# Self-attention with the score matrix built twice: once for its maxima, once with keys on partitions

## The chip, the cores and the metric

One NeuronCore of a Trainium2 chip runs the whole program in one launch. The metric is the device time of one execution in microseconds. The engines are PE (TensorE: matmuls, with its weight loads shown apart), DVE (VectorE), ACT (ScalarE), POOL (GpSimd) and SP (SyncE, which here only issues DMAs).

## The reference

Two blocks follow each other on x of shape (2, 256, 32, 32), in fp32. The first is a deformable attention with a bias network and an MLP; the change leaves it alone. The second is plain self-attention over the 1024 pixels of each image, 8 heads of width 32, so 16 (image, head) pairs:

```python
xf = transpose(x.reshape(B, C, N), (0, 2, 1))            # N = 1024
q, k, v = split((xf @ W_qkv + b_qkv).reshape(B, N, 8, 96), 3, axis=-1)
attn = softmax(einsum('bihd,bjhd->bijh', q, k) * SCALE, axis=2)
res  = einsum('bijh,bjhd->bihd', attn, v).reshape(B, N, 256)
res  = res @ W_out + b_out + xf
```

## The kernel before

Each engine has an instruction stream written out by hand; semaphores tie them together. The first attention, its bias network and the MLP fill the span up to 1027 us. The second attention is what the change rewrites. Its stages before:

1. V product (L1026, added to the bias by DVE in L741): 16 blocks of 128 pixels, all 256 value columns, two fp32 matmuls a block.
2. q and k projections (L1038): 8 products n (which = q or k, t = a block of 128 channels), each of four fp32 512-column matmuls. ACT takes the fp32r rounding of each (L531, semaphore f_hi) and DVE the rest (L767, f_lo). SP writes both parts to DRAM (`send_parts`, L299) and later fetches, for a head, the 32 rows of a part several times under each other (`load_head`, L303 and L304: 8 DMAs of 128 KB), so that one product over 128 rows gives hi*hi + hi*lo + lo*hi + lo*lo. DVE splits V into three bf16 parts meanwhile (`v_part`).
3. The loop: `Fori` over 8 pairs of heads, 16 units in each, 128 units in all. A unit is 128 queries (on partitions) against 1024 keys. PE makes the scores (`scores`, L1047, two 512-column fp32r matmuls), DVE their negated row maximum (`maxes`, L773), ACT the exponential with that bias (L535), PE eight 128x128 transposes of the probabilities (`turn`, L1055), ACT, DVE and POOL the fp16 high and low parts of the result (L540, L543, L776, L779, L390), PE 16 small matmuls with V (`weigh`, L1063), whose last column holds the sum, DVE its reciprocal (L786), ACT the scaling (L550), POOL two adds (L395, L397).
4. PE transposes the results back (L1102), ACT copies them (L574), PE does the output projection (L1113, 32 records), DVE adds bias and input (L814), SP stores (L327).

A matmul of two fp32 operands appears in the trace as two records; a fp32r one as one. Where the output lies in 32 of 128 partitions ("128*32" in a row), four such matmuls run side by side in the array: the layer-3 product of the bias network (L907) is of that form.

PSUM has 8 banks of 512 fp32. Before, scores of unit u lie in banks 2(u%2) and the next, so they are double buffered.

Of the kernel before, what the change touches and what calls it, by code (L numbers as in the profile page):

```python
# [7 lines left out]
P = 128  # L8
# [7 lines left out]
KD = 8  # L16
# [41 lines left out]
def build(nc, d, out):  # L58
# [5 lines left out]
    with ctx:  # L64
# [14 lines left out]
        k_d = dram("k_d", [2, G * D, N], fp32)  # L79

# [8 lines left out]
        qw = sb("qw", [P, CT, P])  # L89
        kw = sb("kw", [P, CT, P])  # L90
        vw = sb("vw", [P, CT, P])
        outw = sb("outw", [P, CT, C])
        m1 = sb("m1", [P, CT, 4 * C])
# [6 lines left out]
        conv = sb("conv", [P, T * 9, KD])  # L100
        gel = sb("gel", [P, T * 9, KD])
# [23 lines left out]

        gb = m1[:, :, :]
# [34 lines left out]
        def v(name, i=0, n=1):  # L161
# [32 lines left out]
        st_in = [sem("st_in0"), sem("st_in1")]  # L194
        sc_ready, mx_ready, pr_ready, pT_ready, pTh_ready, pTl_ready, oo_ready, oo_saved = (
            sem(x) for x in ("sc_ready", "mx_ready", "pr_ready", "pT_ready", "pTh_ready", "pTl_ready", "oo_ready", "oo_saved"))
        pF_ready, pFh_ready, pFl_ready = sem("pF_ready"), sem("pFh_ready"), sem("pFl_ready")
        v_done = sem("v_done")
        sums_column, o_sum, o_done = sem("sums_column"), sem("o_sum"), sem("o_done")
        rT_ready, rT_saved, fin_ready, fin_saved, stored = (  # L200
            sem(x) for x in ("rT_ready", "rT_saved", "fin_ready", "fin_saved", "stored"))
# [26 lines left out]
        def _(sp):  # L228
# [946 lines left out]
```

## Time and profile before

| | us |
|---|---|
| median of 3 runs | 1402.4 (1402.36 to 1404.89) |
| profiled execution, its own time | 1401.21 |
| its span in the profile | 1399.0 |
| PE busy | 1302.2 (93%) |
| ACT busy | 967.6 (69%) |
| DVE busy | 921.5 (66%) |
| POOL busy | 748.9 (54%) |
| V product begins (L1026) | 1027.11 |
| first scores (L1047) | 1073.88 |
| output projection begins (L1113) | 1381.88 |

Times inside the profile are counted from the start of the span; 2.2 us of the execution lie outside it. A busy PE is not a PE at its peak: the durations of matmuls overlap, so what one costs is the distance between starts. "issue" in a chain is time in which an engine waited for nothing that the profile shows.

### The profile page before, as it was taken

To read this page: it belongs to the slowest core of one execution; us is meant where nothing else is said; L and a number is where in the kernel's file an instruction comes from. 1 tells how busy PE (TensorE), PEld (TensorE's weight loads), DVE (VectorE), ACT (ScalarE), POOL (GpSimd) and SP (SyncE) were. 2 spreads that over 40 slices of the span, in tenths; PEclk is the share of its full clock that TensorE was granted. 3 is DMA by queue.
4 is the path that set the end of the run, shared out by engine and by line. 5 is a ranking of instruction groups with operands and counts; after the bars stand their busy time and mean duration, and the time that the engine had idled before them with its cause. 6 is when DMAs were issued, how large, how long until landed. Compare 5 with 4: busy or idle time off the path is not lost.

```text
span 1399.0 us, 29958 instructions
## 1 busy us (share of the span) xinstructions
PE 1302.2 (93%) x11666; PEld 616.0 (44%) x11666; DVE 921.5 (66%) x1270; ACT 967.6 (69%) x1263; POOL 748.9 (54%) x681
## 2 busy tenths in 40 slices
PE   3169999999999999999999998799997999999998
PEld 2132222222222222222222226444454888888885
DVE  6876666666666666666666657410037999999995
ACT  3377777777777777777777773332204999999994
POOL 4166666666666666666666652200000767777772
PEclk9579999999999999999999999999999999999999
DMA  2141110111011101110111000000007222212211
GB/s 69 54 134 31 31 32 2 31 31 32 2 31 32 29 4 32 31 26 7 31 32 23 9 1 1 1 0 0 0 29 272 62 60 60 54 45 52 60 30 60
DMA packets 19922, 53.27 MB, mean 38 GB/s; under 512 B 4642, under 2 KB 7330, under 8 KB 19668
## 3 DMA queue, kind: packets, MB, share of 16 engines
q1 hardware_dynamic: 19824, 51.92, 14.1%
q8 instruction: 70, 1.15, 0.4%
q14 instruction: 24, 0.20, 0.0%
q10 hardware_dynamic: 4, 0.01, 0.0%
HBM read 40.95 MB, written 10.95 MB: 37 GB/s over the span
## 4 chain that ended last, share of the span: by engine, by line
PE 80%; DVE 11%; issue 3%; ACT 2%; POOL 2%; DMA 1%; SPq 1%; DVEq 0%; ACTq 0%; POOLq 0%
PE ps L898 31%; PE ps L907 17%; PE ps L889 5%; DVE aneg L773 5%; PE ps L1055 4%; PE ps L1063 4%; PE ps L1004 4%; PE ps L1014 4%; PE ps L1047 3%; DVE conv L620 2%; PE ps L1038 1%; DVE big L776 1%; POOL big L355 1%; PE ps L1026 1%; PE ps L991 1%
## 5 line engine op out<-in xcount | busy, mean ns | idle before, releaser
L898 PE MATMUL ps<-big,w 64*64 64x512 f32 x4096 | 483.5, 589 | 0.0
L479 ACT ACTIVATE big<-ps 128x1024 f32<-128x1024 f32 x256 | 262.0, 1023 | 179.0 <-PE ps L898 179.0
L674 DVE TENSOR_SCALAR big<-big 128x1024 f32<-128x1024 f32 x256 | 177.8, 694 | 263.8 <-POOL big L370 263.8
L668 DVE TENSOR_TENSOR big<-qpad,ps 128x1024 f32<-128x1024 f32 x256 | 311.0, 1215 | 7.8 <-ACT ps L458 5.4
L370 POOL TENSOR_TENSOR big<-qpad 128x1024 f32<-128x1024 f32 x128 | 244.5, 1910 | 133.2 <-PE ps L898 68.6
L370 POOL TENSOR_TENSOR big<-qpad,V 128x1024 f32<-128x1024 f32 x128 | 244.5, 1910 | 129.7 <-PE ps L898 73.5
L479 ACT ACTIVATE big<-ps,vec 128x1024 f32<-128x1024 f32 x256 | 284.0, 1109 | 0.0
L390 POOL TENSOR_TENSOR big<-BT,big 128x512 f16<-128x512 f32 x129 | 150.4, 1166 | 248.0 <-DVE big L776 248.0
L907 PE MATMUL ps<-big,w3s 128*32 128x512 f32 x2048 | 246.2, 598 | 1.3 <-ACT big L479 1.3
L898 PEld LDWEIGHTS ps<-big,w 64*64 64x64 f32 x4096 | 146.6, 133 | 205.9 <-issue 112.6
L773 DVE TENSOR_REDUCE aneg<-ps 128x1 f32<-128x1024 f32 x131 | 158.3, 1209 | 6.0 <-PE ps L1047 5.7
L535 ACT ACTIVATE big<-ps,aneg 128x1024 f32<-128x1024 f32 x130 | 148.5, 1142 | 6.0 <-DVE aneg L773 5.3
L1055 PE MATMUL ps<-ident,big 128*128 128x128 f32 x1032 | 136.3, 274 | 3.8 <-DVE big L779 3.8
L907 PEld LDWEIGHTS ps<-big,w3s 128*32 128x32 f32 x2048 | 53.5, 109 | 181.7 <-ACT big L479 92.2
L1055 PEld LDWEIGHTS ps<-ident,big 128*128 128x128 f32 x1032 | 121.1, 141 | 23.2 <-DVE big L779 5.7
L1063 PE MATMUL ps<-BT,big 128*128 x2048 | 115.6, 208 | 1.1
L1063 PEld LDWEIGHTS ps<-BT,big 128*128 128x128 f16 x2048 | 99.0, 97 | 21.3 <-issue 10.3
L889 PE MATMUL ps<-S,wl 57*64 57x512 bf16 x1024 | 102.3, 389 | 1.5 <-ACT vs L474 1.5
L1047 PE MATMUL ps<-h1l,h1h 128*128 128x512 f32 x262 | 94.5, 443 | 6.8 <-DMA h1l<-k_d 5.2
L889 PEld LDWEIGHTS ps<-S,wl 57*64 57x64 bf16 x1024 | 29.5, 105 | 144.7 <-ACT big L479 80.7
L779 DVE SCALAR_TENSOR_TENSOR big<-ps,big 128x512 f16<-128x512 f32 x129 | 89.1, 691 | 0.8 <-ACT big L543 0.4
L540 ACT ACTIVATE BT<-ps 128x512 f32<-128x512 f32 x129 | 79.1, 613 | 4.0 <-PE ps L1055 4.0
(140 smaller groups left out, 1116.5 us busy)
## 6 DMA issues: line engine op xcount, KB each, us to landing
raw<-s_f SPq DMA_DIRECT2D x32, 512.0 KB, 6.1
h1h<-q_d SPq DMA_DIRECT2D x64, 128.0 KB, 3.0
h1l<-k_d SPq DMA_DIRECT2D x64, 128.0 KB, 3.1
q_d<-XN SPq DMA_DIRECT2D x8, 512.0 KB, 2.6
k_d<-XN SPq DMA_DIRECT2D x8, 512.0 KB, 2.6
X<-in_x SPq DMA_DIRECT2D x2, 1024.0 KB, 6.3
out<-X SPq DMA_DIRECT2D x8, 256.0 KB, 2.0
m<-grid_d SPq DMA_DIRECT2D x1, 1024.0 KB, 4.6
```

The costliest lines, as they stand in the source:

```text
L370: pool.tensor_tensor(h1[m % HRING].rearrange("p (y a b) -> p y a b", y=2, b=W), u.unsqueeze(2).to_broadcast(shape), a[:, :, HALF // W * hf ...
L390: pool.tensor_tensor(PTL[u % 2][:, 0:HALF], PF[u % 2], PTH[u % 2][:, 0:HALF], ALU.subtract).then_inc(pFl_ready, 1)
L479: act.activation(h2[m % H2RING], z2[m % ZRING], ACT.Relu, bias=v("cb2") if m % 2 else 0.0).then_inc(h2_ready, 1)
L535: act.activation(PR[u % 2], bank(2 * (u % 2), 2), ACT.Exp, bias=aneg[u % 2][:, :]).then_inc(pr_ready, 1)
L668: dve.tensor_tensor(h1[m % HRING].rearrange("p (y a b) -> p y a b", y=2, b=W), u.unsqueeze(2).to_broadcast(shape), b[:, :, HALF // W * hf: ...
L674: dve.tensor_scalar(h1[m % HRING], h1[m % HRING], 0.0, None, ALU.max).then_inc(h1_ready, 1)
L773: dve.tensor_reduce(aneg[u % 2][:, :], bank(2 * (u % 2), 2), AX.X, ALU.max, negate=True).then_inc(mx_ready, 1)
L889: pe.matmul(z2[m % ZRING][CH * y:CH * (y + 1), HALF * x:HALF * (x + 1)], wl1[CH * x:CH * x + KROWS, 2 * w + y, :], S[CH * x:CH * x + KROWS ...
L898: last = pe.matmul(z2[m % ZRING][CH * y:CH * (y + 1), HALF * x:HALF * (x + 1)], w2[CH * x:CH * (x + 1), :], h1[m % HRING][CH * x:CH * (x + ...
L907: last = pe.matmul(zb[32 * k:32 * (k + 1), :], w3s[:, a:a + 32], h2[(m + k // 2) % H2RING][:, HALF * (k % 2):HALF * (k % 2 + 1)], start=(m ...
L1055: last = pe.transpose(bank(4 + hf)[:, P * i:P * (i + 1)], PR[u % 2][:, P * jt:P * (jt + 1)], ident[:, :])
L1063: last = pe.matmul(bank(6 + u % 2)[:, 0:VW], pT[u % 2][:, P * jt:P * (jt + 1)], V3[:, 2 * k + u // NK, jt, :], start=(jt == order[0] and p ...
```

## The change

The transposes of the probabilities, the fp16 parts, the bf16 parts of V and the final transposes go. The second attention becomes this, over 128 slots (16 heads x 8 blocks), all written out with no `Fori`:

- `along(x)`: scores with queries on partitions (query i of block `it` is number 8i + it, so the stationary operand is read with a stride of 8), three stacked products (96 rows) in place of four, always in banks 0 and 1. It serves only for the negated maxima (`maxes`), kept as 8 columns a head.
- POOL splits a head's maxima into a fp32r part and the rest; SP writes them to DRAM and reads them back as two rows of 1024 (`move_max`), rows 96 and 97 of the head's query operand; the key operand holds ones there.
- `across(s)`: the same scores again, keys on partitions, 98 rows, so that the product already has the maximum subtracted; banks 2 and 3 or 4 and 5. ACT takes the exponential straight from there into a ring of 6 (`PT`).
- `weigh(p)`: 8 fp32 matmuls of 256 columns, four side by side, first with V (128x32), then with ones (128x32), which gives the sums. `divide(n)`: a reciprocal of 128x256 and a multiplication for each head, whose result SP places with four DMAs (`place_head`).
- PE's order in slot s: `across(s)`, `along(s + 13)`, and in odd slots `weigh(s - 3)` and `weigh(s - 2)`. Thirteen `along` stand ahead of slot 0, the first eight with two V blocks (`value`) before each.
- Heads 0, 1 and 2 are loaded at first (6 DMAs each); head n + 2 is loaded in iteration n of SP's loop, after the last `across` of head n - 1.
- The projections come ahead of the V product now, and SP sends only four of the eight parts before it loads heads. In the first block the tiles qw, kw, conv and gel share space with others, and the late weights are fetched after k_ready.

```diff
-Q_STACK, K_STACK = [0, 0, 1, 1], [0, 1, 0, 1]
-VW = 3 * D + 1
-PSCALE = 2.0 ** 12
+Q_STACK, K_STACK = [0, 0, 1], [0, 1, 0]
+ROWS = D * len(Q_STACK)
+HEADS3, PRING, AHEAD_MAX = 3, 6, 13
+QUARTER = N // 4
 WS_POOL = 4
-UNITS = 2 * NK
+SLOTS = G * NK
 
...
-        QS = [h1h[:, 2 * i:2 * i + 2, :].rearrange("p a b -> p (a b)") for i in range(2)]
+        QS = [h1h[:, 2 * i:2 * i + 2, :].rearrange("p a b -> p (a b)") for i in range(2)] + [qk3[:, 0, :]]
+        KS = [h1l[:, 2 * i:2 * i + 2, :].rearrange("p a b -> p (a b)") for i in range(2)] + [qk3[:, 1, :]]
+        PT = [big[:, 4 + i, :] for i in range(PRING)]
+        OT = [big[:, 10, QUARTER * i:QUARTER * (i + 1)] for i in range(2)]
+        orec = [big[:, 10, QUARTER * i:QUARTER * (i + 1)] for i in (2, 3)]
+        amax = [sb(f"amax{i}", [P, NK]) for i in range(HEADS3)]
+        mparts = [sb(f"mparts{i}", [P, 2, NK], fp32r) for i in range(HEADS3)]
...
-            for n in range(6):
+            def load_head(n):
+                i = n % HEADS3
+                for r in range(len(Q_STACK)):
+                    sp.dma_start(QS[i][D * r:D * (r + 1), :].bitcast(fp32), q_d[Q_STACK[r], D * n:D * (n + 1), :]).then_inc(st_in[i], 16)
+                    sp.dma_start(KS[i][D * r:D * (r + 1), :].bitcast(fp32), k_d[K_STACK[r], D * n:D * (n + 1), :]).then_inc(st_in[i], 16)
+            def move_max(n):
+                sp.wait_ge(m_lo, n + 1)
+                sp.dma_start(m_d[n].rearrange("a (q t) -> q a t", t=NK), mparts[n % HEADS3][:, :, :].bitcast(fp32)).then_inc(m_out, 16)
+                sp.wait_ge(m_out, 16 * (n + 1))
+                sp.dma_start(QS[n % HEADS3][ROWS:ROWS + 2, :].bitcast(fp32), m_d[n]).then_inc(m_in, 16)
+            def place_head(n):
+                sp.wait_ge(o_done, n + 1)
+                row, t = D * (n % HP), n // HP
+                for c in range(4):
+                    sp.dma_start(rT[row:row + D, t, QUARTER * c:QUARTER * (c + 1)], OT[n % 2][D * c:D * (c + 1), :]).then_inc(rT_in, 16)
+            for n in range(4):
                 send_parts(n)
             for i in range(2):
-                sp.wait_ge(parts_out[i], 32 * 3)
-            load_head(0, 0)
-            load_head(1, 1)
-            for n in range(6, 2 * T):
+                sp.wait_ge(parts_out[i], 32 * 2)
+            for n in range(HEADS3):
+                load_head(n)
+            for n in range(4, 2 * T):
                 send_parts(n)
             for i in range(2):
                 sp.wait_ge(parts_out[i], 32 * T)
-            with sp.Fori(0, G // 2 - 1) as k:
-                sp.wait_ge(sc_ready, UNITS * k + NK)
-                load_head(0, 2 * k + 2)
-                sp.wait_ge(sc_ready, UNITS * k + 2 * NK)
-                load_head(1, 2 * k + 3)
-            sp.wait_ge(sc_ready, UNITS * (G // 2 - 1) + NK)
-            sp.sem_inc(st_in[0], 16 * 2 * HP)
+            move_max(0)
+            for n in range(1, G):
+                if n + 2 < G:
+                    if n >= 2 or n + 2 >= HEADS3:
+                        sp.wait_ge(st_ready, NK * (n + 2 - HEADS3 + 1))
+                    load_head(n + 2)
+                move_max(n)
+                place_head(n - 1)
+            place_head(G - 1)
...
+            pool.memset(ones[:, :], 1.0).then_inc(ones_ready, 1)
+            pool.wait_ge(ones_ready, 1)
+            for i in range(HEADS3):
+                pool.tensor_copy(KS[i][ROWS:ROWS + 2, :], ones[ROWS:ROWS + 2, 0:1].to_broadcast((2, N))).then_inc(ones_ready, 1)
+            pool.wait_ge(ones_ready, 1 + HEADS3)
+            for n in range(G):
+                pool.wait_ge(mx_ready, NK * (n + 1))
+                if n >= HEADS3:
+                    pool.wait_ge(m_out, 16 * (n - HEADS3 + 1))
+                hi, lo = (mparts[n % HEADS3][:, a, :] for a in range(2))
+                pool.tensor_copy(hi, amax[n % HEADS3][:, :]).then_inc(m_hi, 1)
+                pool.wait_ge(m_hi, n + 1)
+                pool.tensor_tensor(lo, amax[n % HEADS3][:, :], hi.bitcast(fp32), ALU.subtract).then_inc(m_lo, 1)
...
+            for s in range(SLOTS):
+                act.wait_ge(st_ready, s + 1)
+                if s >= PRING:
+                    act.wait_ge(pv_done, s - PRING + 1)
+                act.activation(PT[s % PRING], bank(2 + 2 * (s % 2), 2), ACT.Exp).then_inc(pr_ready, 1)
...
+            def maxes(x):
+                n, it = x // NK, x % NK
+                dve.wait_ge(sc_ready, x + 1)
+                if it == 0 and n >= HEADS3:
+                    dve.wait_ge(m_lo, n - HEADS3 + 1)
+                dve.tensor_reduce(amax[n % HEADS3][:, it:it + 1], bank(0, 2), AX.X, ALU.max, negate=True).then_inc(mx_ready, 1)
+            def divide(n):
+                dve.wait_ge(pv_done, NK * (n + 1))
+                dve.reciprocal(orec[n % 2], bank(6 + n % 2)[:, QUARTER:2 * QUARTER]).then_inc(rec_done, 1)
+                dve.wait_ge(rec_done, n + 1)
+                if n >= 2:
+                    dve.wait_ge(rT_in, 64 * (n - 1))
+                dve.tensor_tensor(OT[n % 2], bank(6 + n % 2)[:, 0:QUARTER], orec[n % 2], ALU.mult).then_inc(o_done, 1)
...
+            for x in range(NK):
+                value(2 * x)
+                value(2 * x + 1)
+                maxes(x)
+            for x in range(NK, SLOTS + 2 * NK):
+                if x < SLOTS:
+                    maxes(x)
+                n = (x - NK - AHEAD_MAX - 1) // NK
+                if n >= 0 and (x - NK - AHEAD_MAX - 1) % NK == 0:
...
+            def along(x):
+                n, it = x // NK, x % NK
+                if it == 0:
+                    pe.wait_ge(st_in[n % HEADS3], 96 * (n // HEADS3 + 1))
+                if x >= 1:
+                    pe.wait_ge(mx_ready, x)
+                for hf in range(2):
+                    last = pe.matmul(bank(hf), QS[n % HEADS3][0:ROWS, it:it + NK * (P - 1) + 1:NK],
+                                     KS[n % HEADS3][0:ROWS, HALF * hf:HALF * (hf + 1)], start=True, stop=True)
+            def across(s):
+                n, kt = s // NK, s % NK
+                if kt == 0:
+                    pe.wait_ge(m_in, 16 * (n + 1))
+                if s >= 2:
+                    pe.wait_ge(pr_ready, s - 1)
+                for hf in range(2):
+                    last = pe.matmul(bank(2 + 2 * (s % 2) + hf), KS[n % HEADS3][0:ROWS + 2, P * kt:P * (kt + 1)],
+                                     QS[n % HEADS3][0:ROWS + 2, HALF * hf:HALF * (hf + 1)], start=True, stop=True)
+                last.then_inc(st_ready, 1)
+            def weigh(s):
+                n, kt = s // NK, s % NK
+                if kt == 0 and n >= 2:
+                    pe.wait_ge(o_done, n - 1)
+                pe.wait_ge(pr_ready, s + 1)
+                for a, w in enumerate((V[:, n, kt, :], ones[:, :])):
+                    for c in range(4):
+                        last = pe.matmul(bank(6 + n % 2)[D * c:D * (c + 1), QUARTER * a:QUARTER * (a + 1)], w,
+                                         PT[s % PRING][:, QUARTER * c:QUARTER * (c + 1)],
+                                         start=(kt == 0 and a == 0), stop=(kt == NK - 1), skip_group_check=True)
+                last.then_inc(pv_done, 1)
+            for x in range(NK):
+                value(2 * x)
+                value(2 * x + 1)
+                along(x)
+            for x in range(NK, AHEAD_MAX):
+                along(x)
+            pe.wait_ge(vv_saved, 2 * NK)
+            pe.wait_ge(ones_ready, 1 + HEADS3)
+            for s in range(SLOTS + 2):
+                if s < SLOTS:
+                    across(s)
+                if s + AHEAD_MAX < SLOTS:
+                    along(s + AHEAD_MAX)
+                if s % 2 == 1:
+                    for p in (s - 3, s - 2):
+                        if p >= 0:
+                            weigh(p)
+            pe.wait_ge(mx_ready, SLOTS)
+            pe.wait_ge(pr_ready, SLOTS)
```

## Rows read from the trace of the kernel before

**Rows 1.** Page, chain that ended last: shares of the span by engine.

```profile
PE 80%; DVE 11%; issue 3%; ACT 2%; POOL 2%; DMA 1%; SPq 1%; DVEq 0%; ACTq 0%; POOLq 0%
```

**Rows 2.** Windows, loop of 128 units: length, busy per engine (instructions), clock, DMA.

```profile
1085.00:1370.00 285.00, 280.64 (x3221) 242.22 (x3219) 275.15 (x497) 277.19 (x496) 200.87 (x370) 1.00 0.22 52
```

**Rows 3.** Timeline inside the loop: start, duration, engine, line, operation.

```profile
1203.11 0.71 PE L1047 MATMUL ps<-h1l,h1h 128*128 128x512 f32 x2
...
1203.31 1.13 ACT L535 ACTIVATE big<-ps,aneg 128x1024 f32<-128x1024 f32 x1
...
1203.66 1.03 PE L1055 MATMUL ps<-ident,big 128*128 128x128 f32 x8
...
1203.91 1.20 DVE L773 TENSOR_REDUCE aneg<-ps 128x1 f32<-128x1024 f32 x1
...
1204.64 0.87 PE L1063 MATMUL ps<-BT,big 128*128 x16
...
1205.34 0.71 PE L1047 MATMUL ps<-h1l,h1h 128*128 128x512 f32 x2
```

**Rows 4.** Timeline, end of a pair of heads, where DVE waited for scores.

```profile
1360.18 0.72 PE L1047 MATMUL ps<-h1l,h1h 128*128 128x512 f32 x2
...
1360.94 1.23 DVE L773 TENSOR_REDUCE aneg<-ps 128x1 f32<-128x1024 f32 x1 [0.32 <-PE ps L1047]
```

**Rows 5.** Timeline, bias network: a 128*32 burst and what follows it.

```profile
500.52 1.92 PE L907 MATMUL ps<-big,w3s 128*32 128x512 f32 x16
502.37 0.41 PE L889 MATMUL ps<-S,wl 57*64 57x512 bf16 x4
```

**Rows 6.** DMA issues: out<-in, count, size of one, median us from issue to landing.

```profile
h1h<-q_d SPq DMA_DIRECT2D x64, 128.0 KB, 3.0
...
q_d<-XN SPq DMA_DIRECT2D x8, 512.0 KB, 2.6
...
vec<-in_vecs SPq DMA_DIRECT2D x1, 41.0 KB, 1.9
...
grid_d<-gxy SPq DMA_DIRECT2D x1, 8.0 KB, 2.5
```

**Rows 7.** Timeline, start of the second attention.

```profile
1027.11 14.08 PE L1026 MATMUL ps<-qpad,X 128*128 128x256 f32 x64 [0.84 <-DVE X L736]
...
1056.11 1.28 DVE L767 SCALAR_TENSOR_TENSOR XN<-ps,vec,XN 128x1024 fp32r<-128x1024 f32 x1 [1.01 <-ACT XN L531]
...
1066.97 0.35 SPq L303 DMA_DIRECT2D h1h<-q_d  x1
...
1073.88 2.04 PE L1047 MATMUL ps<-h1l,h1h 128*128 128x512 f32 x4 [5.23 <-DMA h1l<-k_d]
1074.32 0.90 SPq L299 DMA_DIRECT2D q_d<-XN  x2
```

**Rows 8.** Windows around the wait before the first scores.

```profile
1068.50:1071.00 2.50, 0.15 (x1) 0.00 (x0) 1.49 (x2) 2.29 (x2) 0.00 (x0) 1.00 0.94 252
...
1078.00:1080.00 2.00, 2.00 (x9) 1.70 (x9) 1.20 (x1) 0.96 (x2) 0.00 (x0) 0.50 1.03 416
```

**Rows 9.** Timeline, end of the first attention: a shorter idle time of PE.

```profile
892.66 1.09 PE L978 MATMUL ps<-ident,big 128*128 128x128 f32 x4 [2.30 <-POOL big L377]
```

**Rows 10.** Window right behind it.

```profile
893.00:894.00 1.00, 0.75 (x4) 0.34 (x2) 0.82 (x2) 1.00 (x2) 0.07 (x1) 0.50 0.00 0
```

**Rows 11.** Groups by form: busy us, mean ns, idle before.

```profile
L1026 PE MATMUL ps<-qpad,X 128*128 128x256 f32 x64 | 14.1, 381 | 0.8 <-DVE X L736 0.8
...
L786 DVE RECIPROCAL arec<-ps 128x1 f32<-128x1 f32 x128 | 20.2, 158 | 0.0
...
L713 DVE RECIPROCAL srec<-ssum 128x8 f32<-128x8 f32 x16 | 3.1, 196 | 0.0
...
L741 DVE TENSOR_TENSOR big<-ps,bv 128x256 f32<-128x256 f32 x16 | 6.8, 425 | 7.8 <-PE ps L1026 7.8
```

**Rows 12.** Timeline, the output projection at the end.

```profile
1381.88 13.90 PE L1113 MATMUL ps<-XN,qpad 128*128 128x512 f32 x32
```

More of the change, by code:

```diff
@@ L124, in build @@
         vs = sb("vs", [P, T, 2, 2 * D])
+        conv, gel = (big[:, i, 0:T * 9 * KD].rearrange("p (a b) -> p a b", b=KD) for i in (10, 11))
         gb = m1[:, :, :]
@@ L736, in _, with value @@
                     dve.scalar_tensor_tensor(xs, bank(4 + r % 4), v("mlp_b2", ct), xs, ALU.add, ALU.add).then_inc(x2_ready, 1)
-            for n in range(2 * NK):
+            def value(n):
                 b, jt = n // NK, n % NK
@@ L1020, in _ @@
             wv = wqkv[:, :, :].rearrange("p t (k n) -> p t k n", k=3)
-            for n in range(2 * NK):
-                b, jt = n // NK, n % NK
-                if n >= 4:
-                    pe.wait_ge(vv_saved, n - 3)
-                for kt in range(CT):
-                    last = pe.matmul(bank(4 + n % 4)[:, 0:C], X[:, CT * b + kt, P * jt:P * (jt + 1)], wv[:, kt, 2, :],
-                                     start=(kt == 0), stop=(kt == CT - 1))
-                last.then_inc(vv_ready, 1)
             pe.wait_ge(qw_scaled, 2)
@@ L1040, in _ @@
                 last.then_inc(p_ready, 1)
-            def scores(u):
-                i, it = u // NK % 2, u % NK
-                for jh in range(2):
-                    last = pe.matmul(bank(2 * (u % 2) + jh), QS[i][:, P * it:P * (it + 1)], KS[i][:, HALF * jh:HALF * (jh + 1)],
-                                     start=True, stop=True)
-                last.then_inc(sc_ready, 1)
-            def turn(u, hf):
-                for i in range(4):
-                    jt = 4 * hf + i
-                    last = pe.transpose(bank(4 + hf)[:, P * i:P * (i + 1)], PR[u % 2][:, P * jt:P * (jt + 1)], ident[:, :])
-                last.then_inc(pT_ready, 1)
@@ L1058, in weigh @@
-            def weigh(u, k):
-                order = list(range(4, NK)) + list(range(4))
-                for jt in order:
-                    for pT in (PTH, PTL):
-                        last = pe.matmul(bank(6 + u % 2)[:, 0:VW], pT[u % 2][:, P * jt:P * (jt + 1)],
-                                         V3[:, 2 * k + u // NK, jt, :],
-                                         start=(jt == order[0] and pT is PTH), stop=(jt == order[-1] and pT is PTL))
-                last.then_inc(oo_ready, 1)
@@ L1094, in _, with value @@
[L1094 to L1105 removed]
+            def value(n):
+                b, jt = n // NK, n % NK
+                if n >= 4:
+                    pe.wait_ge(vv_saved, n - 3)
+                for kt in range(CT):
+                    last = pe.matmul(bank(4 + n % 4)[:, 0:C], X[:, CT * b + kt, P * jt:P * (jt + 1)], wv[:, kt, 2, :],
+                                     start=(kt == 0), stop=(kt == CT - 1))
+                last.then_inc(vv_ready, 1)
```

186 lines of the change are left out of this document (15 added, 171 removed).

## The prediction

> **What bounds the kernel now.** I read the page's chain first: 80% of what ended last is PE [rows 1], and up to 1027 us the change touches none of it. So I read the second attention alone. The windows of its loop show PE busy 280.6, ACT 277.2 and DVE 275.2 of 285 us at clock 1.00 [rows 2]: three engines are full together. In the timeline the scores of two units start at 1203.11 and 1205.34 [rows 3]; over the loop a unit takes about 2.2 us. PE spends them as 0.55 us from scores to transposes, 0.98 on transposes and 0.70 on the product with V, by starts [rows 3]. That is the price to beat, 2.2 us a unit, 128 times; a rewrite that only lifts ACT and DVE gains nothing, if PE or a chain of waits then takes 2.4.
>
> **The change part by part.** I rebuild the timeline from 1027.11, where the V product begins [rows 7], and add the terms.
>
> *Start.* The projections move ahead of the V product, so they begin 13.9 us earlier. The rest of part 3 (L767, started at 1056.11, 1.28 us) ends then at 1043.5 instead of 1057.4 [rows 7]; its DMA lands 2.6 us later [rows 6], at 1046.1. SP now loads three heads: 18 DMAs. Before, 16 of them stood between 1066.97 and 1074.32 [rows 7], 0.46 us each, so 18 hold SP for 8.3 us, till 1054.4, and the parts 4 to 7 are queued behind them. The data: 18 x 128 KB at the 252 GB/s of such loads [rows 8] flow till 1055.8 at the earliest, I take 1057, then four half-megabyte parts at about 416 GB/s [rows 8] until 1062, landed at 1063. ACT reuses the buffer of part 5 for part 7 only then, about 1.1 us, and DVE's rest takes 1.28 [rows 7]. PE waits for all rests: it starts on V at 1065.4, after an idle time of 10 us. Without that jam it would be 1057; with faster loads 1062.
>
> *The thirteen `along` ahead.* V costs 14.08 us for 16 blocks [rows 7, 11], 0.88 a block, and a pair of fp32r matmuls 0.43 (two records that together last 0.71, the last of them with its latency) to 0.55 (the distance to the next form [rows 3]); I take 0.45. Eight rounds of two blocks and one `along`: 8 x 2.2 = 17.7. The banks 0 and 1 are single now, so an `along` waits for the maximum of the one ahead: scores start at 1360.18, DVE at 1360.94, for 1.23 us [rows 4], and with some 0.05 to the release that is a chain of 2.04 us from `along` to `along`. Five more: 10.2. PE restarts cold: before, after 5.23 us of idleness [rows 7] it still ran at clock 0.50 between 1078 and 1080, up to 6 us later [rows 8]. Of 6 us at half speed 3.1 are lost, gaps and edges estimated. Slot 0 begins at 1065.4 + 17.7 + 10.2 + 3.1 = 1096.4.
>
> *A pair of slots.* `weigh` has the form of L907, whose burst of 16 records of 512 columns holds PE for 1.85 us including the change of array form [rows 5]; two `weigh` are 32 records of half the length, so 1.85 again (bounds 1.72, with no overhead, and 2.0, with the overhead of L907 for each group of four). PE's order per pair is: `along` (odd x), `across`, `along` (even x), two `weigh`, `across`. The first `along` and the second stand 2.04 us apart by the chain of the maximum, although PE has only one `across` of 0.45 to do between them: about 1.1 us of PE idle. After the second come 0.45 + 1.85 + 0.45 = 2.75 us, which covers its own maximum. The period is 2.04 + 2.75 = 4.8, with changes of form 4.85: 2.43 us a slot, more than the 2.2 before. Bounds: 4.66 (1.72 for the weights) and 5.14 (0.55 per pair of matmuls, 2.0). ACT has one exponential a slot, 1.13 us [rows 3], and hides. 115 slots also hold an `along`: 57.5 x 4.85 = 278.9 (bounds 268 to 296). The last 13 have none: 6.5 x 2.75 = 17.9. Pair 0 has no `weigh` and one pair stands after the last slot: +1.0.
>
> *Head boundaries.* Slot 8n needs `m_in`(n), the maxima of its head. They are known six slots earlier, but SP issues `move_max`(n) behind `load_head`(n + 2), which waits for `across`(8n - 1): the slot just before. From its end: six issues of 0.46 = 2.8 us; the maxima out, an 8 KB DMA of 256 short pieces, like grid_d 2.5 us; back in again 1.9 to 2.5 [rows 6]. That is 7.2 to 7.8 if the small DMA passes the six loads. The last load is issued at 2.5 and lands 3.0 later, at 5.5 [rows 6]; if the small one follows it, it lands at 6 to 7 and slot 8n starts at 8 to 9. I take 8.2. PE's own cover from the end of `across`(8n - 1): the rest of the 2.04 chain, an `along` and two `weigh`, 3.3 us. Stall 4.9 us (bounds 4.0 and 5.7). n = 1 to 13 have it; heads 14 and 15 have no load ahead of `move_max`, so SP is not held. 13 x 4.9 = 63.7 (52 to 74).
>
> The Trainium skill, in "DMA: Bandwidth & Descriptors", "Queues, rings and completion order", says that descriptors of SP's DMAs are consumed in ring order on each DMA engine. By that rule the maxima wait behind the loads and the upper half of my bounds holds (about +0.5 us each, +6 in all); no row shows a small DMA behind loads.
>
> *The clock after each stall.* After 5.23 us idle PE came back at 0.50 [rows 7, 8], and after 2.30 us as well (restart 892.66, 0.50 in the window behind it) [rows 9, 10]. A stall of 4.9 may therefore end at half speed. In the 6 us behind it the pair loses 2 to 2.5 us (the matmuls double, the idle of the maximum chain takes part of it back). I count 1.6 us a boundary: 13 x 1.6 = 20.8 (0 to 33).
>
> *`divide`.* It follows the maximum of an even x, waits for the `weigh` of its head and so sits just ahead of the next maximum, with no slack. Reciprocals of 1 and 8 elements take 158 and 196 ns [rows 11], 5.4 ns an element, so 256 cost about 1.5 us; the multiplication is like L741, 0.42 [rows 11]. It starts at 4.65 of the period, ends at 6.7, and the maximum that could have begun at 5.65 is 1.05 late: 14 heads x 1.05 = 14.7 (0, if the reciprocal runs like L741, to 24).
>
> The Trainium skill, "VectorE: DVE Perf Modes", "First, the fixed hardware budget", has the reciprocal as an iterated divide with a repeat count of 8, which speaks against the change. Read as 8 cycles of its 0.96 GHz for each element that would be an estimate of 2.1 us in place of 1.5 and 14 x 0.6 = 8 us more; the two short rows fit neither value well.
>
> *End.* The output projection starts at 1381.88, 17.1 us ahead of the span's end [rows 12]. The first image's four groups (6.9 us) hide the last `divide` (2.0), its four issues and a landing. The 8 transposes that stood ahead of it, some 3.6 us, are gone; that is in the sum since I start from the last `weigh`. POOL's two operations of 128x8 lie in the six slots of lead. The earlier edits (shared tiles, late weights after k_ready) I put at nothing: the raw load of the next group is needed tens of us later; if not, 1 to 2 us.
>
> *Sum.* 1096.4 + 278.9 + 17.9 + 1.0 + 63.7 + 20.8 + 14.7 = 1493.4; + 17.1 = 1510.5 us of span. The execution was 2.2 longer than its span, and the median is 1.2 above that execution: 1513.9, 8% over 1402.4.
>
> **The rivals.**
> 1. *The boundaries are cheap* (SP's chain fits better than I read, the clock holds, the reciprocal is short). For it: the maxima are ready early, and two of three terms rest on a single kind of row. Half of the stalls gone, no cold clock, no `divide` term: 1514 - 32 - 21 - 15 = 1446, up to 1480 if one of them stays. Chance 0.19.
> 2. *PE heavier than L907 suggests*: 256-column matmuls need a weight load for every 107 ns of columns. Were a `weigh` 1.3 us, a pair would be 5.6 and the time 1514 + 57.5 x 0.75 + 6.5 x 0.75 = 1562. Against it: L907's loads leave gaps. Chance 0.08.
> 3. *Not slower: no wait at the boundary at all*, i.e. the maxima come back inside PE's 3.3 us of cover. Its price is 64 + 21: 1429. It decides for "not slower" from a pair of 4.4 us on (57.5 x 0.45 = 26), where 4.08, twice the maximum chain, is the floor: the weights would have to pass in under 1.4 us a pair. Against it: six issues alone take 2.8 us. Chance 0.06, most of it faster.
>
> **How the numbers follow.** My forecast (1480 to 1550) has 0.67. Leaving out rival 2's far part and rival 3 and the lowest of rival 1 gives 1450 to 1546 for 8 in 10; the bounds of the terms alone give 1460 to 1545. A difference under 0.2% can't be told from none here: faster 0.05, same 0.02, slower 0.93.
>
> **What would show it.** In the profile after: V starting near 1065 behind an idle PE; `along` to `along` alternating 2.04 and 2.8 us, PE waiting for the maximum once a pair; at every eighth `across`, 13 times, PE waiting 4 to 6 us for a DMA of maxima, with six loads issued right before it, and clock 0.50 behind it; a reciprocal of 1.5 us or more; ACT and DVE near half busy. I am wrong if PE doesn't stop at the boundaries, if the pair is under 4.5 us, or if the maxima overlap the next `along`.

## The result and the profile after

| | before | after |
|---|---|---|
| median us (runs) | 1402.5 | 1557.3 (1553.1 to 1559.3, 4 runs) |
| ratio, 95% interval | 1 | 1.110 [1.107, 1.112] |
| profiled execution, its span | see above | 1553.1, 1551.3 |
| mean granted clock | 0.974 | 0.922 |

The change makes the kernel slower by 155 us; 1513.9 was forecast, and 1557.3 is 11 us above 1546, the upper end of the range. The direction, the places and the kinds of waits were right. Two sizes were too low, the pair of slots and the clock; a third, the stall, was too high and hid part of that.

The page of the changed kernel, its busy line, its clock line and its chain (to be set against [rows 1]):

```profile
PE 1348.9 (87%) x10852; PEld 552.8 (36%) x10852; DVE 808.5 (52%) x905; ACT 800.7 (52%) x867; POOL 546.2 (35%) x331
PEclk8589999999999999999999989998778888878889
PE 79%; DVE 9%; DMA 5%; SPq 3%; POOL 2%; issue 2%; ACT 1%; DVEq 0%; ACTq 0%; POOLq 0%
```

The clock line is the one to look at. From the fourth slice to the 27th it stands at 9, but for one 8; from the 28th (it begins at 1047 us), in which V and the second attention start, it falls to 7 and 8. DMA and SP's queue, together 8%, are in a chain of a kernel that moves little data: somebody waits for small transfers.

The start, from the timeline (start, length, engine, line, operation; in brackets the idle time ahead of it and who ended it):

```profile
1062.57 1.11 ACT L529 ACTIVATE XN<-ps,vec 128x1024 fp32r<-128x1024 f32 x1 [12.13 <-DMA q_d<-XN]
1067.50 3.78 PE L971 MATMUL ps<-qpad,X 128*128 128x256 f32 x8 [11.35 <-DVE XN L729]
1099.54 1.06 PE L995 MATMUL ps<-h1h,h1l 98*128 98x512 f32 x2
```

ACT waits 12.13 us for the stores that are queued behind the eighteen loads, and PE waits for ACT and DVE. V starts at 1067.5 (1065.4 was forecast) and slot 0 at 1099.5 (1096.4). Among the `along` ahead of slot 0 stands this row:

```profile
1095.93 1.25 PE L983 MATMUL ps<-h1l,h1h 96*128 96x512 f32 x2 [1.32 <-DVE amax L713]
```

Five of these `along` wait 1.3 to 1.4 us each for a maximum. From the third of them on, at 1093, the granted clock is 0.50, and it stays there to 1112, in the first slots.

An undisturbed pair of slots:

```profile
1201.70 0.74 PE L995 MATMUL ps<-h1h,h1l 98*128 98x512 f32 x2
1202.27 0.66 PE L983 MATMUL ps<-qk 96*128 96x512 f32 x2
1202.77 0.63 PE L995 MATMUL ps<-h1h,h1l 98*128 98x512 f32 x2
1202.97 1.23 DVE L713 TENSOR_REDUCE amax<-ps 128x1 f32<-128x1024 f32 x1 [1.80 <-PE ps L983]
1204.25 0.87 PE L983 MATMUL ps<-qk 96*128 96x512 f32 x2 [0.85 <-DVE amax L713]
1205.05 0.64 PE L1007 MATMUL ps<-big 128*32 128x256 f32 x8
1206.92 0.74 PE L995 MATMUL ps<-h1h,h1l 98*128 98x512 f32 x2
```

L983 is `along`, L995 `across`, L1007 `weigh`. The pair lasts 5.22 us. From the first `along` to the second 1.98 us pass, since the second waits for the maximum; from there to the weights 0.80; the two `weigh` take 1.87; the `across` ahead of the next `along` 0.57. PE stands still once a pair although nothing is short of work: the order gives it too little to do between two `along`.

A head boundary and the `divide` behind it, SP's queue and the engines:

```profile
1208.62 0.32 SPq L298 DMA_DIRECT2D h1h<-q_d  x1
1211.30 0.42 SPq L304 DMA_DIRECT2D m_d<-mparts  x1
1214.92 0.24 SPq L306 DMA_DIRECT2D h1h<-m_d  x1
1216.43 1.22 PE L995 MATMUL ps<-h1h,h1l 98*128 98x512 f32 x2 [4.25 <-DMA h1h<-m_d]
1224.70 1.76 DVE L718 RECIPROCAL big<-ps 128x256 f32<-128x256 f32 x1 [2.38 <-PE ps L1007]
1226.49 0.43 DVE L722 TENSOR_TENSOR big<-ps,big 128x256 f32<-128x256 f32 x1
1226.83 1.21 DVE L713 TENSOR_REDUCE amax<-ps 128x1 f32<-128x1024 f32 x1
1228.19 0.91 PE L983 MATMUL ps<-h1l,h1h 96*128 96x512 f32 x2 [1.57 <-DVE amax L713]
1229.03 1.08 PE L1007 MATMUL ps<-big 128*32 128x256 f32 x8
```

SP issues the six loads from 1208.62 on, the maxima leave at 1211.30, and only 3.6 us later has SP seen them land and can issue their way back, which takes 1.5 us. The 3.6 are among the longest: over the thirteen boundaries it is 2.4 to 3.9, in the mean 3.0. PE starts again at 1216.43 after 4.25 us. Three slots on, the reciprocal and the multiplication stand ahead of a maximum, and PE waits 1.57 us for that one. The windows around both gaps (length, then busy time and count of PE, PEld, DVE, ACT and POOL, the granted clock, the DMA share and GB/s):

```profile
1212.00:1216.00 4.00, 0.18 (x4) 0.00 (x0) 0.00 (x0) 0.00 (x0) 0.00 (x0) 0.90 0.27 52
1216.00:1218.00 2.00, 1.57 (x4) 1.29 (x5) 0.00 (x0) 0.32 (x1) 0.00 (x0) 0.50 0.00 0
1226.00:1228.00 2.00, 0.62 (x3) 0.19 (x1) 1.97 (x3) 1.68 (x2) 0.00 (x0) 1.00 0.00 0
1228.00:1230.00 2.00, 1.81 (x14) 1.08 (x18) 0.91 (x2) 0.00 (x0) 0.39 (x2) 0.71 0.22 52
1230.00:1232.00 2.00, 2.00 (x24) 0.88 (x20) 0.36 (x1) 0.00 (x0) 0.00 (x0) 0.50 0.07 17
1150.00:1350.00 200.00, 147.55 (x1082) 82.82 (x1081) 80.75 (x68) 54.03 (x55) 2.74 (x14) 0.81 0.14 33
```

The granted clock is 0.50 (1.2 of 2.4 GHz) behind the stall, which I had forecast. It falls a second time, behind the gap that the `divide` leaves, which I had not, but not in each head: in 8 of 13, behind gaps of 1.31 to 1.94 us. In the other five it held, behind gaps of 1.19 to 1.96, as here, where the eight matmuls of a weight group still pass in 0.64 us and not in 1.08:

```profile
1432.13 0.84 PE L983 MATMUL ps<-h1l,h1h 96*128 96x512 f32 x2 [1.19 <-DVE amax L713]
1432.90 0.64 PE L1007 MATMUL ps<-big 128*32 128x256 f32 x8
```

Over 200 us of the loop the clock is 0.81. The waits from 1100 to 1520 (total us, times, longest), all of PE:

```profile
PE ps L983 <- DVE amax L713: 53.8, 59, 2.0
PE ps L995 <- DMA h1h<-m_d: 33.8, 9, 4.2
PE ps L995 <- DMA qk<-m_d: 15.1, 4, 4.5
```

The two DMA rows are the thirteen boundaries: 48.9 us, 3.76 each (3.4 to 4.5).

### The profile page after: what moved, and what is told of

Read it like the earlier page. It is cut to its first block, busy times and chain, and to the rows that moved or that the text cites. A ratio compares the mean times of both kernels' runs of the same rounds, so it can differ in the third digit from the quotient of the medians.

```text
span 1551.3 us, 25531 instructions
## 1 busy us (share of the span) xinstructions
PE 1348.9 (87%) x10852; PEld 552.8 (36%) x10852; DVE 808.5 (52%) x905; ACT 800.7 (52%) x867; POOL 546.2 (35%) x331
## 4 chain that ended last, share of the span: by engine, by line
PE 79%; DVE 9%; DMA 5%; SPq 3%; POOL 2%; issue 2%; ACT 1%; DVEq 0%; ACTq 0%; POOLq 0%
PE ps L830 28%; PE ps L839 15%; PE ps L1007 8%; PE ps L983 5%; PE ps L821 5%; DVE amax L713 4%; PE ps L936 4%; PE ps L946 4%; PE ps L995 3%; DMA m_d<-mparts 2%; DVE big L582 2%; DVE big L718 1%; SPq L299 1%; SPq L298 1%; PE ps L923 1%
## 5 line engine op out<-in xcount | busy, mean ns | idle before, releaser
L477 ACT ACTIVATE big<-ps 128x1024 f32<-128x1024 f32 x256 | 261.9, 1023 | 178.9 <-PE ps L830 178.9
L536 ACT ACTIVATE big<-ps 128x1024 f32<-128x1024 f32 x128 | 127.4, 1023 | 337.2 <-PE ps L995 337.1
L713 DVE TENSOR_REDUCE amax<-ps 128x1 f32<-128x1024 f32 x128 | 156.6, 1224 | 220.1 <-PE ps L983 219.6
L983 PE MATMUL ps<-h1l,h1h 96*128 96x512 f32 x176 | 78.4, 532 | 42.5 <-DVE amax L713 42.5
L995 PE MATMUL ps<-h1h,h1l 98*128 98x512 f32 x176 | 70.8, 493 | 33.8 <-DMA h1h<-m_d 33.8
L1007 PE MATMUL ps<-big 128*32 128x256 f32 x1024 | 98.2, 462 | 0.0
L1007 PE MATMUL ps<-big,ones 128*32 128x256 f32 x1024 | 96.0, 453 | 0.0
L983 PEld LDWEIGHTS ps<-h1l,h1h 96*128 96x128 f32 x176 | 50.8, 328 | 67.9 <-DVE amax L713 44.8
L698 DVE SCALAR_TENSOR_TENSOR X<-ps,vec,X 128x512 f32<-128x512 f32 x8 | 6.0, 751 | 105.0 <-PE ps L946 105.0
L518 ACT ACTIVATE big<-ps,vec 128x512 f32<-128x512 f32 x32 | 22.0, 687 | 73.0 <-PE ps L936 73.0
```

Source lines behind the costliest of these rows:

```text
L477: act.activation(h2[m % H2RING], z2[m % ZRING], ACT.Relu, bias=v("cb2") if m % 2 else 0.0).then_inc(h2_ready, 1)
L536: act.activation(PT[s % PRING], bank(2 + 2 * (s % 2), 2), ACT.Exp).then_inc(pr_ready, 1)
L713: dve.tensor_reduce(amax[n % HEADS3][:, it:it + 1], bank(0, 2), AX.X, ALU.max, negate=True).then_inc(mx_ready, 1)
L983: last = pe.matmul(bank(hf), QS[n % HEADS3][0:ROWS, it:it + NK * (P - 1) + 1:NK], KS[n % HEADS3][0:ROWS, HALF * hf:HALF * (hf + 1)], start ...
L995: last = pe.matmul(bank(2 + 2 * (s % 2) + hf), KS[n % HEADS3][0:ROWS + 2, P * kt:P * (kt + 1)], QS[n % HEADS3][0:ROWS + 2, HALF * hf:HALF ...
L1007: last = pe.matmul(bank(6 + n % 2)[D * c:D * (c + 1), QUARTER * a:QUARTER * (a + 1)], w, PT[s % PRING][:, QUARTER * c:QUARTER * (c + 1)], ...
```

## The experiments

My theory after the result: the excess over the parent comes from the order of the work, that is from SP's queue at the boundaries, from the `divide` ahead of a maximum, from the clock that falls behind PE's gaps, and from two `weigh` together where one behind each `along` would cover the maximum. The rival: the work itself is too heavy for PE (scores computed twice, a row of ones beside V), and mending waits brings little. That the clock can fall twice a head I learned only from experiments 1 and 2. Medians are in us, ratios are to the parent timed beside each; the numbers below are an order for reading, in part not that of the runs. Ahead of the projections all these kernels are the same, yet in their traces the projections began anywhere from 1027.7 to 1032.0 us. So where a difference is small, it is also given by stages of the trace.

**1. The maxima ahead of the loads.** In SP's loop `move_max(n)` is issued before the wait for `across`(8n - 1) and the six loads:

```
+                move_max(n)
                 ... (wait, load_head(n + 2))
-                move_max(n)
```

> Only the order in SP's loop is changed: move_max(n) stands ahead of the wait for the last across of head n - 1 and the six loads. Theory: the 13 stalls of 4.2 us come from that order, and the cold clock behind them from the stalls. A head period is 29.3 us in the changed kernel; four undisturbed pairs are 20.85 and a divide at full clock costs 1.07, so 21.9 should be left, 13 x 7.4 = 96 us less: 1461 us, no wait of PE for a DMA of maxima, clock near 1.00. Rival (the two landings of the maxima are too slow wherever they are issued, or the clock falls by PE's small gaps alone): at most 30 us less, above 1525.

Measured: 1473.9 (1472.7 to 1475.6), ratio 1.048 [1.044, 1.053]: 83 us less than the change. PE no longer waits for maxima from DRAM. SP's rows of this kernel show the way out of the maxima without six loads ahead of it:

```profile
1205.83 0.74 SPq L304 DMA_DIRECT2D m_d<-mparts  x1
1207.79 0.24 SPq L306 DMA_DIRECT2D qk<-m_d  x1
```

1.96 us from issue to issue in this head; over thirteen heads it is 2.2 in the mean (1.6 to 3.0), where the change has 3.0. The stalls themselves were 48.9 of the 83 us. The other 34.5 (2.65 a boundary) are put down to pairs that now run at full clock; by the traces, in which a head takes 23.23 us in place of 29.30 and 3.76 of that was the stall, it is 2.3 a boundary. It ended 13 us above the 1461 that I expected, and the reason is in the rows: in 11 of 13 heads the clock still falls, in the gap of the `divide`:

```profile
1226.51 1.05 PE L983 MATMUL ps<-h1l,h1h 96*128 96x512 f32 x2 [1.94 <-DVE amax L713]
1227.49 1.08 PE L1007 MATMUL ps<-big 128*32 128x256 f32 x8
1150.00:1350.00 200.00, 160.43 (x1365) 95.13 (x1364) 103.28 (x87) 68.82 (x70) 3.52 (x18) 0.94 0.16 39
```

Eight weight matmuls in 1.08 us instead of 0.64 are half speed; the window's clock is 0.94. The head before this one is one of the two in which the clock held, behind a gap of the same length:

```profile
1204.61 0.84 PE L983 MATMUL ps<-h1l,h1h 96*128 96x512 f32 x2 [1.95 <-DVE amax L713]
```

**2. PE kept busy in the stall.** Twenty score matmuls into a free bank ahead of the wait at each of the 13 boundaries, with the maxima as late as in the change:

```
+                    if 1 <= n < G - 2:
+                        for i in range(10): (two matmuls of 512 columns into across's own banks)
                     pe.wait_ge(m_in, 16 * (n + 1))
```

> The stalls stay, but PE computes 20 more score matmuls of 512 columns (into the banks that the slot then overwrites) at each of the 13 boundaries while it waits for the maxima. Theory: idle time of PE lowers the clock, and what that costs is 2.9 us in the first pair and 1.6 in the second of a head, so 13 x 4.5 = 59 us come back with the stall itself unchanged: 1498 us. Rival (the longer first pairs are not the clock's doing, or the clock falls all the same by the smaller gaps): 1540 to 1560.

Measured: 1539.5 (1537.9 to 1541.9), ratio 1.095 [1.090, 1.100]: 18 us less than the change, far fewer than I expected. The trace says why:

```profile
1221.53 1.22 PE L983 MATMUL ps<-h1l,h1h 96*128 96x512 f32 x2 [1.95 <-DVE amax L713]
1222.67 1.08 PE L1012 MATMUL ps<-big 128*32 128x256 f32 x8
```

The clock survives the stall (1.00 from 1214 to 1221) and falls a little later, in 12 of 13 heads, in the gap of 1.95 us in front of the `divide`'s late maximum (0.51 from 1221 to 1226). One cover of two doesn't do. Besides, the twenty matmuls hold PE for about 4.7 us, 0.9 more than the mean stall, which is 12 of the missing 41 us.

**3. The `divide` two slots later.** Where the count of maxima x is compared, AHEAD_MAX + 1 becomes AHEAD_MAX + 3, so that the `weigh` it waits for is long past:

```
-                n = (x - NK - AHEAD_MAX - 1) // NK
+                n = (x - NK - AHEAD_MAX - 3) // NK
```

> The reciprocal and multiplication of a head stand behind the maximum of two slots later, so they do not wait for the weights' product and have 1.78 us of DVE's idle time before the next maximum. Theory: the delay of 1.07 us at full clock shrinks to about 0.4, and without the gap of 1.6 us in PE the second fall of the clock (1.6 us a head) is rarer: 13 x (0.7 to 2.3) = 9 to 30 us less, 1527 to 1548. Rival (DVE's work is hidden, the second cold pair comes from the stall alone): 1550 to 1558.

Measured: 1529.9 (1527.8 to 1533.2), ratio 1.088 [1.083, 1.093]: 27 us less, within the 9 to 30 expected. The lateness of the maximum is 14 x 1.07 = 15 at most, since two waits of a head stay 0.1 and 0.24 us longer than those of an undisturbed pair. The boundaries' stalls are as before (49.6 us in all), the window's clock rose from 0.81 to 0.88, and behind the `divide`, with a gap of 1.1 us now, it no longer falls in any head: that is the rest, 12 us or a little more.

**4. Both covers.** Experiments 2 and 3 together.

> Both edits of e2_filler and e3_divide_later on the changed kernel: the stalls of the boundaries stay, filled with 20 score matmuls, and the divide stands two slots later. e2 gained 18 us in place of 59, since the clock fell a moment later at the divide's gap of 1.95 us. Theory: the clock has two places per head to fall, and one fall costs about the same wherever it is; with both closed the head period is 20.85 + 0.4 + a stall of 4.3: 25.6 in place of 29.3, 1509 us, clock above 0.97 between 1150 and 1450. Rival (the two edits only add up): 1557 - 18 - 27 = 1512 with the clock well under 0.97; the clock of the stretch and not the time tells them apart.

Measured: 1509.3 (1506.7 to 1512.0), ratio 1.075 [1.073, 1.077], as expected, and the clock is full:

```profile
1225.40 4.83 PE L996 MATMUL ps<-qk 96*128 96x512 f32 x20
1230.09 0.74 PE L1000 MATMUL ps<-qk 98*128 98x512 f32 x2
1150.00:1350.00 200.00, 170.96 (x1400) 112.23 (x1399) 91.88 (x79) 61.69 (x63) 3.15 (x16) 1.00 0.14 34
```

This separates the clock from the waits: the boundaries still cost their time (4.7 us of filling from start to start, 0.9 more than the mean stall of 3.76), yet 48 us are gone. In the traces a head takes 25.69 us, 3.61 less than in the change. Take off 0.7 for the `divide`, whose gap is shorter now, add 0.9 for the filling's surplus, and the clock alone cost 3.6 to 3.8 us a head.

**5. Experiments 1 and 3 together.**

> Both edits of e1_max_first and e3_divide_later: the maxima move before the loads, the divide stands two slots later. In e1 the clock still fell once a head, right behind the gap of 1.94 us that the divide leaves in PE. Theory: with that gap down to about 1.3 us the clock holds, and a head costs four pairs of 5.21 and 0.4: 14 x 1.7 us less than e1, 1448 us, clock above 0.97 in the stretch. Rival (the clock falls by PE's gaps of 0.85 us in every pair as well): 1458 to 1468, clock as in e1.

Measured: 1451.2 (1450.1 to 1454.6), ratio 1.033 [1.030, 1.036], 3 us above what I expected. The window's clock is 0.98: behind the `divide`, with a gap of 1.07 to 1.10 us, it fell in 4 of 13 heads and held in nine. What remains over the parent timed beside it is 47 us. The pairs are of that size: 57.5 x (5.22 - 4.4) = 47, with 4.4 for two units of the parent [rows 3]. That the two agree is partly luck: in the traces slot 0 starts 25 us after the parent's first scores, and from there to the output projection 334.5 us pass against the parent's 308.0, in which every eighth unit is longer (2.6 or 2.9 us) and makes the mean 2.31.

**6. The stationary queries of `along` contiguous.** In the change they are every eighth column of QS; here a block of 128, so the maxima belong to other queries.

```
-                    last = pe.matmul(bank(hf), QS[n % HEADS3][0:ROWS, it:it + NK * (P - 1) + 1:NK],
+                    last = pe.matmul(bank(hf), QS[n % HEADS3][0:ROWS, P * it:P * (it + 1)],
```

> along reads its stationary queries contiguously (block it = queries 128 it to 128 it + 127) in place of a stride of 8 elements; the maxima then belong to other queries than the rows say, which leaves the amount of work as it was. Theory: the weight load of 328 ns falls to the 190 ns of the kernel before, and since the first along of a pair waits for a maximum its load is exposed: 0.14 us a pair, 57 pairs, 8 us less, 1549; along to weigh goes from 0.80 to 0.66 us. Rival (the load is slow because it waits for the matmul ahead of it, not by its stride): same, within 3 us.

Measured: 1547.3 (1540.2 to 1550.2), ratio 1.100 [1.094, 1.106]: 10 us less. An undisturbed pair of its trace takes 5.05 us in place of 5.22, 0.17 less, of which 0.14 lie between `along` and the weights (0.66 for 0.80). Once more on the best order below, see 9.

**7. One `weigh` a slot**, on top of experiment 1:

```
-                if s % 2 == 1:
-                    for p in (s - 3, s - 2):
-                        if p >= 0:
-                            weigh(p)
+                if s >= 2:
+                    weigh(s - 2)
```

> The kernel of e1 with one weigh(s - 2) in every slot in place of two in every odd one. Theory: the pair is long because one of its two maximum chains (1.98 us) has only an across behind it; with a weigh behind each, a slot takes PE's own 0.57 + 0.52 + 1.01 = 2.1 us, with the chain just hidden: 115 x (2.61 - 2.1) = 58 us less than e1, 1416 us. Rival (PE's time per slot is what it is and changes of array form cost more than the gap did): within 10 us of e1, 1464 to 1484.

Measured: 1415.0 (1412.4 to 1416.6), ratio 1.007 [1.004, 1.009]: 59 us less than experiment 1, and the window's clock is 1.00, though the `divide` stands where it stood: now at most 0.8 us of waiting is left behind it (14 waits, 10.9 us). The rival (PE too heavy) falls here: no pass was taken away, only reordered.

**8. The start, then the `divide` in two.** First, on top of 7, SP sends six parts out, loads head 0, sends the last two parts and loads the other heads. Then, on top of that, the reciprocal follows one maximum and the multiplication the next.

```
-            for n in range(4):
+            for n in range(6):
...
-            for n in range(HEADS3):
+            load_head(0)
+            for n in range(6, 2 * T):
+                send_parts(n)
+            for n in range(1, HEADS3):
                 load_head(n)
-            for n in range(4, 2 * T):
-                send_parts(n)
```

> e6_one_weigh with SP sending six parts before it loads head 0, and the last two before heads 1 and 2. Theory: ACT's wait for the landing of parts 4 and 5 (12.1 us, behind 18 loads) goes; the V product starts at about 1058.6 in place of 1067.5 and less cold: 9 to 11 us less than e6. Rival (the first scores wait for their head instead): at most 3 us less.

Measured: 1404.4 (1401.9 to 1405.0), ratio 1.000 [0.9985, 1.0006], 10.7 us less than 7. V starts 8.5 us earlier than in 7 (1070.72), behind an idle time of 2.52 us in place of 11.10, and runs its first blocks less cold:

```profile
1062.26 1.99 PE L972 MATMUL ps<-qpad,X 128*128 128x256 f32 x8 [2.52 <-DVE XN L730]
```

```
+                    for f, at in ((invert, NK + AHEAD_MAX + 1), (divide, NK + AHEAD_MAX + 2)):
+                        if x >= at and (x - at) % NK == 0 and (x - at) // NK < G:
+                            f((x - at) // NK)
```

> e7_start with reciprocal and multiplication behind two successive maxima. Theory: DVE is free for about 0.85 us in a slot of 2.1, so 2.15 us in one place delay the next maximum by 1.3 us and 1.76 only by 0.9: 14 x 0.4 = 6 us less than e7. Rival (the reciprocal is hidden in the slot or the delay is caught up by PE): within 2 us of e7.

Measured: 1398.1 (1396.4 to 1400.0), ratio 0.995 [0.994, 0.997], 6 us less, as expected; from V to the output projection the traces have 5.1 less. A slot is now:

```profile
1200.76 0.74 PE L999 MATMUL ps<-qk 98*128 98x512 f32 x2
1201.33 0.69 PE L987 MATMUL ps<-h1l,h1h 96*128 96x512 f32 x2
1201.96 0.64 PE L1011 MATMUL ps<-big 128*32 128x256 f32 x8
1202.06 1.22 DVE L714 TENSOR_REDUCE amax<-ps 128x1 f32<-128x1024 f32 x1 [0.98 <-PE ps L987]
1202.41 0.61 PE L1011 MATMUL ps<-big,ones 128*32 128x256 f32 x8
1202.96 0.50 PE L999 MATMUL ps<-qk 98*128 98x512 f32 x1
```

0.57 `across`, 0.63 `along`, 1.00 `weigh`: 2.20 us, without a wait of PE, against a chain of the maximum of about 2.0. It equals the parent's 2.2 [rows 3]; with the one longer slot of each head, eight slots take 18.2 us here and eight units of the parent 18.5. So what can be gained is mostly at the edges.

**9. Two sequels of 8.** `AHEAD_MAX` 11 instead of 13 (fewer `along` ahead of slot 0, where each waits for its maximum), and, apart from it, the contiguous queries of experiment 6.

```
-HEADS3, PRING, AHEAD_MAX = 3, 6, 13
+HEADS3, PRING, AHEAD_MAX = 3, 6, 11
```

> e8_split with 11 scores ahead in place of 13. Theory: ahead of slot 0 an along costs 2.0 to 2.2 us (the maximum's chain, PE idle), inside a slot about 0.6: 2 x 1.5 = 3 us less, 1395 us, if the maxima still come in time: 4 slots of 2.2 less the maximum's own 1.9 leave 6.9 us for POOL's 0.5 and the two landings of 1.9 to 3.6 and 1.5. Rival (SP is busy with place_head when they are ready): PE waits for m_d once a head, 14 x 1 us or more, 1408 us or above.

Measured: 1394.2 (1392.7 to 1396.0), ratio **0.9927 [0.9913, 0.9941]**: the fastest version that computes all of the reference, faster than both kernels (0.7% under the parent). From V to the output projection it is 4.3 us shorter than 8 (3 expected). Ahead of slot 0 only one `along` of the three that wait is at half clock.

> e8_split with the stationary queries of along read contiguously; the maxima then belong to other queries than the rows say, the amount of work is the same. In e8 a slot is 2.2 us, PE alone: 0.57 across, 0.62 along, 1.0 weigh. Theory: part of the along's 0.62 is its longer weight load; it falls to the 0.57 of across: 115 x 0.05 = 6 us less, 1392 us. Rival (a load that starts ahead of its turn is hidden whatever its length): within 2 us of 1398.

Measured: 1388.2 (1385.8 to 1390.5), ratio 0.988 [0.986, 0.990]: again 10 us less (9.2 from V to the output projection, 6 expected), by a reason that the groups of the trace show, ahead of the contiguous queries (experiment 8) and with them (line, engine, form and count, busy us, mean ns, idle):

```profile
L987 PEld LDWEIGHTS ps<-h1l,h1h 96*128 96x128 f32 x128 | 36.1, 331 | 10.6 <-issue 5.6
```

```profile
L987 PEld LDWEIGHTS ps<-h1l,h1h 96*128 96x128 f32 x130 | 23.7, 188 | 11.9 <-issue 6.8
```

The same load, 96x128 elements, takes 331 ns with a stride of eight elements and 188 ns without one. Even with no wait ahead of it, the excess of the load isn't fully hidden: 9 to 10 us over 115 `along` are 0.08 to 0.09 a slot.

## Why the prediction was wrong

**What bounds it.** Right: three full engines became one chain of PE with waits, DVE and ACT near half busy (52% each), and the transposes' departure bought nothing.

**The start.** Right. The idle of PE was 11.35 us (10 forecast); the forecast is 3.1 us too low at slot 0, of which 1.3 lie ahead of the projections. That the earlier edits, put "at nothing", cost them is not shown: later traces, with the same code up to there, begin the projections from 0.7 us earlier to 3.6 us later. Experiment 8 gives back the part that SP's order costs.

**A pair of slots: the step that failed first.** The 0.45 us taken for a pair of fp32r matmuls, out of 0.43 to 0.55, was used for each of `along` and `across`. Chain and weights held: 1.98 (2.04) and 1.87 (1.85). But the two `across` and `along` around them took 0.57 and 0.80 instead of 0.45 and 0.45. With an edge of 0.06 in the forecast and the chain 0.06 shorter that is 5.22 for 4.85, and 57.5 x 0.37 = 21 us. I had taken the bare columns, though the distance to the next form, 0.55, stood in [rows 3] as the upper end. For `along` even that was low. It has a strided load of 328 ns, and here the load stands directly behind the wait for the maximum, so nothing covers it:

```profile
L983 PEld LDWEIGHTS ps<-h1l,h1h 96*128 96x128 f32 x176 | 50.8, 328 | 67.9 <-DVE amax L713 44.8 <-issue 19.5
```

Experiment 6 shows 0.17 us of this a pair, 0.14 of it at this `along`; the rest of its 0.35 over the forecast (a shorter load still stands behind the wait, and the form changes) was not tried by itself. The last 13 slots show the same without `along`: 2.98 a pair for 2.75 (starts 1514.44 and 1517.42), 1.5 us in all.

**The boundaries.** Right in mechanism and in place (13 times, with six loads ahead), too high in size: 3.76 us each for 4.9, below even the lower bound of 4.0, and 48.9 for 63.7. The slot began 7.3 us in the mean (7.0 to 8.0) after SP's first load, not 8.2, and PE came to the wait 0.3 later than I thought. Experiment 1 shows the cause: only the order of two calls in SP's queue. The rule that the Trainium skill gives in "DMA: Bandwidth & Descriptors", "Queues, rings and completion order", is that on each DMA engine the descriptors of a ring are consumed in order. The trace does not speak against it: the maxima's way out takes 3.0 us in the mean behind six loads and 2.2 without them. But what I worked out of it, the upper half of my bounds, did not come, and whether the 0.8 us is the ring's order or the loads' share of the bandwidth was not separated.

**The clock: the step that failed second, and the larger one.** "I count 1.6 us a boundary." From restart to restart a head took 29.30 us in the mean (1127.71, the first stall's end, to 1479.30, the thirteenth's, by 12). Four pairs are 20.85 of it, the stall 3.76, the `divide` 1.07; 3.6 are left for the clock, 47 us in thirteen heads, where I had 20.8 and 33 as the upper bound. Experiments 1 and 4 confirm it from outside: 2.3 a boundary by 1, in whose heads another 1.3 remain behind the `divide`, and 3.6 to 3.8 by 4. Two things were wrong. I had read a loss of 2 to 2.5 us behind a restart and still counted 1.6. And the forecast had one fall of 6 us where there were often two, the second in 8 of 13 heads, behind a gap of 1.3 to 1.9 us that I priced as mere lateness. I had even read a fall after 2.30 us [rows 9, 10] and applied it only to the longer stall. Stalls, `divide` and clock together: 8.45 us a head for 7.55, 12 us in all (+26 for the clock, -15 for the stalls). In head 0, which ran at 0.50 behind the `along` ahead until 1112, 3 more are left over.

**`divide`.** Right: the maximum is 1.07 us late (1.05 forecast). The reciprocal takes 1.76 us, between my 1.5 from two short rows and the 2.1 estimated from the Trainium skill, "VectorE: DVE Perf Modes", "First, the fixed hardware budget"; the multiplication 0.43.

**The end.** Right: output projection at 1534.08, 17.2 us ahead of the span's end (17.1).

The sum: +3.1 (start), +21 (pairs), +12 (boundaries), +3.2 (head 0), +1.5 (last pairs) = 40.8, the span's distance from 1510.5. (The other 2.6 us to the median come in because the profiled execution was the fastest of the four.) Two terms lay above their own upper bounds, the pair with 5.22 for 5.14 and the clock with 47 for 33. Either of them as forecast would have left the time inside the range, and that the stalls were 15 us too dear was luck that hid part of both.

**The rivals.** Rival 2 fell: a `weigh` is 0.94 us, not 1.3. Rival 1 was the idea of cheap boundaries at 1446 to 1480; experiments 1 and 5 make them cheap, with 1473.9 and 1451.2. Rival 3 priced maxima that come back under cover at 1429; experiment 1 is that case and gives 1473.9, since the 21 us of the pairs and the fall of the clock behind the `divide` stay. For "not slower" it named the pair, and that is where it was decided: experiment 7 brings it to about 4.4. None of the three signs of being wrong that it named appeared: kinds and places of the waits were right, and sizes missed.

## What to carry to other kernels

Where a product frees an engine but puts a result's round trip between two matmuls, count the order before the work: the same instructions in another order (one `weigh` behind each `along`, the maxima ahead of the loads) took 142 of 155 us back. Price a wait of PE twice, once for its length and once for the matmuls behind it at the lower clock, and look at repeated gaps of a little over 1 us too, not only at the longest: no length was found here below which the clock is safe. Take the start-to-start distance of neighbouring forms as the price of a short matmul, and add its weight load where it stands behind a wait.

## What the runs showed of the hardware

- PE's clock can fall to 0.50 behind short gaps, where PE already idles 0.85 us in each pair, and the length of the gap alone does not decide. It fell behind 8 of 13 gaps of 1.19 to 1.96 us in the changed kernel (it held behind three of 1.95 or 1.96), behind 11 of 13 of 1.93 to 1.95 in experiment 1, behind 4 of 13 of 1.07 to 1.10 in experiment 5 and behind none of 1.1 in experiment 3.
- Ahead of slot 0, where each `along` waits 1.3 to 1.4 us for a maximum, the third that waits ran at half clock in the change and in all eleven runs after it. In the loop of experiments 7 to 9, without the pairs' gaps and with no wait for a maximum above 0.8 us, the clock was 1.00 from 1150 to 1350. What exactly decides was not measured.
- A weight load of 96x128 fp32r elements with a stride of eight takes 328 to 331 ns (the change and experiment 8), a contiguous one 188 (the last run of 9).
- From the issue of the small DMA of maxima to the issue that waits for its landing, 3.0 us pass in the mean (2.4 to 3.9) behind six loads of 128 KB on the same queue, and 2.2 (1.6 to 3.0) without them (experiment 1).
- A reciprocal of 128x256 from PSUM takes 1.76 us in the changed kernel, four times the multiplication of that size (0.43).
